# Two down products ahead of the first pieces, the inverse assembly at the head of iteration 0, and key products first in iteration 13

## The reference

```
x = x + attn(xn) + moe(xn)                   # xn = layernorm(x)
attn: q,k,v = split(silu(causal_conv1d(xn @ w_qkv)))   # 16 key heads, 32 value heads, 128 wide
      q,k = l2norm(q), l2norm(k);  beta = sigmoid(xn @ w_b)
      g = -exp(A_log) * softplus(xn @ w_a + dt_bias)
      per token: St = St*exp(g); St += k (v - k St) beta; o = q St
      o = o * rsqrt(mean(o^2)) * norm_weight * silu(xn @ w_z);  attn = o @ w_out
moe:  top 2 of 8 experts by xn @ router_w, each silu(g)*u @ w2, plus a shared expert of width 1024
```

## Time and profile before

| | us |
|---|---|
| median of 3 runs | 1095.32 (1089.68 to 1099.28) |
| profiled execution, whole | 1106.24 |
| its span | 1104.3 |
| TensorE busy | 1030.0 (93%) |
| VectorE busy | 800.5 (72%) |
| ScalarE busy | 633.9 (57%) |
| GpSimd busy | 519.3 (47%) |

### The profile page before, as it was taken

How to read it: one execution, slowest core, us unless ns; L and a number is a source line. 1 busy time by engine, 2 the same in 40 slices (tenths; PEclk the granted TensorE clock), 3 DMA queues, 4 the chain that set the end, 5 groups by cost and what they waited for, 6 DMA issues and landing times.

```text
span 1104.3 us, 22254 instructions
## 1 busy us (share of the span) xinstructions
PE 1030.0 (93%) x8190; PEld 789.7 (72%) x8190; DVE 800.5 (72%) x1469; ACT 633.9 (57%) x1176; POOL 519.3 (47%) x1140
## 2 busy tenths in 40 slices
PE   4889999999789999999999999999999999996897
PEld 4665666578476877777777778777777778783776
DVE  4552332275769898989889898989888988897444
ACT  4341222234557777666767576777767676774453
POOL 4500000266455557383847465564738374735610
PEclk9989999999879999999999999999999999998999
DMA  9933111151132333415152334233241514332121
GB/s 325 398 114 111 48 34 59 54 160 26 44 120 37 125 50 113 97 65 123 46 116 68 96 74 125 44 119 67 96 104 58 123 57 105 75 97 42 24 47 48
DMA packets 183513, 103.16 MB, mean 93 GB/s; under 512 B 155632, under 2 KB 169584, under 8 KB 180080
## 3 DMA queue, kind: packets, MB, share of 16 engines
q1 hardware_dynamic: 181872, 97.55, 32.1%
q0 software_dynamic: 1536, 4.20, 1.1%
HBM read 79.77 MB, written 21.95 MB: 92 GB/s over the span
## 4 chain that ended last, share of the span: by engine, by line
PE 57%; DVE 8%; ACT 7%; issue 4%; POOL 3%; DMA 1%; SPq 0%; ACTq 0%; DVEq 0%
PE rg L1585 9%; PE pj L1416 6%; PE pj L1418 5%; PE pj L1417 5%; PE rg L1568 5%; PE rg L1552 5%; PE rg L1486 4%; DVE nm L1294 3%; PE rg L1560 3%; PE rg L1569 2%; DVE shared_down_or_conv L1257 2%; ACT vn L1229 2%; ACT sqk L1183 2%; PE rg L1488 2%; PE rg L1531 2%
## 5 line engine op out<-in xcount | busy, mean ns | idle before, releaser
L1085 POOL TENSOR_TENSOR rows<-rows,shared_down_or_conv 128x126 f32<-128x126 f32 (+22 forms) x496 | 187.7, 378 | 239.1 <-DMA shared_down_or_conv<-n_scratch 201.5
L1257 DVE SCALAR_TENSOR_TENSOR shared_down_or_conv<-pj,taps,shared_down_or_conv 128x510 f32<-128x510 f32 x372 | 275.5, 744 | 27.5 <-ACT shared_down_or_conv L1135 18.8
L1088 POOL TENSOR_TENSOR rows<-rows 128x126 f32<-128x126 f32 (+22 forms) x496 | 194.8, 393 | 38.9
L1416 PE MATMUL pj<-xhi,whi 128*128 128x512 f32 x376 | 164.1, 437 | 2.4 <-POOL wlo L1065 1.4
L1294 DVE SCALAR_TENSOR_TENSOR nm<-rg,wneg,hidden_or_decays 128x512 f32<-128x512 f32 (+1 forms) x256 | 139.5, 609 | 15.9 <-PE rg L1488 14.1
L1418 PE MATMUL pj<-xhi,wlo 128*128 128x512 f32 x376 | 149.9, 399 | 0.0
L1417 PE MATMUL pj<-xlo,whi 128*128 128x512 f32 x376 | 149.8, 398 | 0.0
L1135 ACT ACTIVATE shared_down_or_conv<-pj,taps 128x512 f32<-128x512 f32 x124 | 85.0, 686 | 108.0 <-PE pj L1418 106.4
L1585 PE MATMUL rg<-wo,gated 128*128 128x256 f32 x512 | 130.6, 391 | 0.1
L1585 PEld LDWEIGHTS rg<-wo,gated 128*128 128x128 f32 x512 | 95.0, 192 | 15.1 <-issue 1.3
L1416 PEld LDWEIGHTS pj<-xhi,whi 128*128 128x128 f32 x376 | 71.5, 190 | 42.7 <-issue 24.4
(11 more groups left out here) (238 smaller groups left out, 1991.3 us busy)
## 6 DMA issues: line engine op xcount, KB each, us to landing
hidden_or_decays<-eg_scratch SPq DMA_DIRECT2D x16, 1536.0 KB, 8.0
wraw<-w_heads SPq DMA_DIRECT2D x16, 776.0 KB, 4.5
w1a<-w_up SPq DMA_DIRECT2D x9, 1024.0 KB, 7.7
shared_down_or_conv<-n_scratch SPq DMA_DIRECT2D x32, 256.0 KB, 4.0
w2a<-w_down SPq DMA_DIRECT2D x8, 512.0 KB
wo<-w_out SPq DMA_DIRECT2D x16, 256.0 KB
n_scratch<-nm SPq DMA_DIRECT2D x64, 64.0 KB
rt_scratch<-shared_down_or_conv SPq DMA_DIRECT2D x32, 128.0 KB, 2.3
```

What stands on the lines that cost most here:

```text
L1085: gp.tensor_tensor(tmp, rb[:, 0:r, t:t + 1].to_broadcast([P, r, w]), nb[:, t:t + 1, t + 1:].to_broadcast([P, r, w]), ALU.mult).then_inc(el ...
L1088: gp.tensor_tensor(rb[:, 0:r, t + 1:], rb[:, 0:r, t + 1:], tmp, ALU.add).then_inc(elim, 1)
L1257: v.scalar_tensor_tensor(out=y, in0=it.pbank[item][:, :, 0:S - s], scalar=taps[par][:, piece(j)[0], KS - 1 - s:KS - s], in1=y, op0=ALU.mul ...
L1416: te.matmul(bank, whi[par][w], xhi[:, k, cols], start=(k == 0), stop=False)
```

## The change

Three parts, each a reordering; no product is added or left out.

1. First block: `down(0)` and `down(1)` stand ahead of the four pieces on TensorE, `down(2)` behind them. On VectorE the softplus parts 1 to 3 leave the loop over products and stand behind it, with `add(0)` and `add(1)` between them, all ahead of the four convolutions.
2. Iteration -1: K comes earlier in TensorE's list; the scans and ScalarE's part of the decays of head 1 (D, E) come here from iteration 0. GpSimd gathers seven sets behind its weight split instead of three. Iteration 0: LA1 is first, the other assembly steps follow closely, the key products come behind them, MIX is VectorE's first item, and GpSimd gathers the last four sets ahead of its weight split.
3. Iteration 13: K0 to K3 stand ahead of LA1, and the output products come later. Iteration 14: SQ is TensorE's first item; Z2, OUT0 and Z3 come ahead of LA1; P4 and P5 stand behind K3 on VectorE.

```diff
--- before.py
+++ after.py
@@ -538,8 +538,8 @@
                         if n == 0:
                             locate()
                             assert count[0] == ROUTED, count
-                        elif n in (2, 5, 6, 7):
-                            softplus((2, 5, 6, 7).index(n))
+                        elif n == 2:
+                            softplus(0)
 
                     def turned_rows(j):
                         v.wait_ge(xt_full, j + 1)
@@ -584,11 +584,13 @@
                                                scalar=-1.0, in1=rk2[:].unsqueeze(2).to_broadcast([P, NT, REP]),
                                                op0=ALU.mult, op1=ALU.mult).then_inc(small, 1)
 
+                    softplus(1)
+                    add(0)
+                    softplus(2)
+                    add(1)
+                    softplus(3)
                     for q in range(4):
                         first_conv(q)
-                        if q == 1:
-                            add(0)
-                    add(1)
                     add(2)
                     turned_rows(0)
                     turned_rows(1)
@@ -739,10 +741,11 @@
                     te.matmul(pR[:, NT * E:2 * NT * E], every[:], either[:], start=True, stop=True).then_inc(counted, 1)
                     for n in range(1, NS):
                         up(n)
+                    for n in range(2):
+                        down(n)
                     for q in range(4):
                         first_project(q)
-                    for n in range(3):
-                        down(n)
+                    down(2)
                     turn_rows(0)
                     turn_rows(1)
                     down(3)
@@ -848,32 +851,33 @@
             LATER = {"G", "H", "DN"}
             OWN = {
                 -1: (
-                    ("K0 G0 K1 H0 G1 K2 H1 K3 P4 G2 H2 P5 G3 H3 P6 DN0 P7 DN1 G4 H4 P0 VT0 VT1 G5 H5 P1 VT2 VT3 G6 H6 P2 "
-                     "G7 H7 P3 DN2 DN3").split(),
-                    ("G0 W G1 P4 G2 P5 S4 G3 P6 S5 SK P7 S6 G4 S7 P0 VT0 VT1 G5 P1 S0 VT2 VT3 G6 P2 S1 G7 P3 S2 S3").split(),
-                    ("K0 K1 H0 K2 H1 K3 P4 H2 P5 H3 P6 DN0 P7 DN1 H4 P0 H5 P1 H6 P2 H7 P3 DN2 DN3").split(),
+                    ("K0 K1 G0 K2 H0 K3 G1 H1 P4 G2 H2 P5 G3 H3 P6 DN0 P7 DN1 G4 H4 P0 VT0 VT1 G5 H5 P1 VT2 VT3 G6 H6 P2 P3 "
+                     "G7 H7 DN2 DN3").split(),
+                    ("G0 W G1 P4 G2 P5 S4 G3 P6 S5 SK P7 S6 G4 S7 P0 VT0 VT1 G5 E0 P1 S0 E1 VT2 VT3 G6 E2 P2 S1 E3 P3 S2 G7 "
+                     "S3").split(),
+                    ("K0 K1 K2 H0 K3 H1 P4 H2 P5 H3 P6 DN0 P7 DN1 H4 D0 P0 D1 H5 D2 P1 D3 H6 P2 P3 H7 DN2 DN3").split(),
                 ),
                 0: (
-                    ("Z0 Z1 P4 P5 SQ Z2 K0 P6 Z3 K1 K2 P7 P0 LA1 K3 LA2 LB1 P1 LB2 U1_0 U1_1 N21_0 N21_1 P2 U2_0 U2_1 "
-                     "VT0 P3 O0 VT1 O1 VT2 O2 O3 VT3").split(),
-                    ("E0 Z0 P4 SQ Z1 S4 P5 S5 E1 P6 E2 W Z2 E3 SK S6 Z3 P7 LA1 LA2 S7 LB1 LB2 U1_0 U1_1 P0 P1 S0 U2_0 P2 "
-                     "U2_1 VT0 S1 O0 P3 O1 VT1 O2 S2 O3 VT2 S3 VT3").split(),
-                    ("D0 P4 D1 D2 P5 SQ D3 K0 P6 K1 K2 P7 K3 MIX N21_0 N21_1 P0 P1 P2 O0 P3 O1 O2 O3").split(),
+                    ("LA1 Z0 Z1 LA2 Z2 P4 LB1 SQ Z3 LB2 K0 P5 U1_0 U1_1 K1 N21_0 N21_1 P6 U2_0 K2 U2_1 K3 P7 O0 P0 O1 P1 "
+                     "VT0 O2 VT1 P2 O3 VT2 P3 VT3").split(),
+                    ("LA1 SQ Z0 Z1 LA2 Z2 P4 LB1 Z3 LB2 S4 W P5 U1_0 U1_1 SK S5 P6 U2_0 U2_1 S6 P7 S7 O0 P0 VT0 S0 O1 P1 "
+                     "VT1 O2 S1 P2 O3 VT2 S2 P3 VT3 S3").split(),
+                    ("MIX P4 SQ K0 P5 K1 N21_0 N21_1 P6 K2 K3 P7 P0 O0 P1 O1 O2 P2 O3 P3").split(),
                 ),
                 NG - 3: (
-                    ("SO Z0 P4 Z1 SQ Z2 K0 OUT0 K1 OUT1 Z3 OUT2 P5 P6 P7 LA1 K2 OUT3 LA2 K3 LB1 OUT4 OUT5 LB2 P0 OUT6 "
-                     "U1_0 U1_1 N21_0 P1 N21_1 U2_0 P2 U2_1 P3 VT0 OUT7 VT1 O0 O1 O2 O3 VT2 VT3").split(),
-                    ("SQ Z0 E0 Z1 P4 Z2 E1 SO Z3 P5 W E2 LA1 S4 E3 LA2 P6 LB1 S5 LB2 P7 S6 U1_0 P0 U1_1 SK S7 P1 U2_0 S0 "
-                     "P2 S1 U2_1 P3 VT0 VT1 S2 O0 O1 O2 O3 VT2 S3 VT3").split(),
-                    ("D0 SO D1 SQ P4 K0 OUT0 OUT1 D2 K1 D3 OUT2 P5 K2 OUT3 K3 P6 OUT4 OUT5 P7 OUT6 N21_0 P0 N21_1 P1 P2 "
-                     "OUT7 P3 O0 O1 O2 O3").split(),
+                    ("SO Z0 Z1 SQ Z2 K0 Z3 K1 P4 K2 P5 OUT0 K3 P6 LA1 OUT1 LA2 P7 LB1 P0 OUT2 LB2 OUT3 U1_0 U1_1 P1 N21_0 "
+                     "N21_1 OUT4 P2 U2_0 U2_1 OUT5 P3 OUT6 VT0 OUT7 VT1 O0 O1 O2 O3 VT2 VT3").split(),
+                    ("SQ E0 Z0 Z1 E1 Z2 E2 SO Z3 E3 P4 W LA1 P5 S4 LA2 P6 LB1 S5 LB2 P7 S6 U1_0 P0 U1_1 SK S7 P1 S0 U2_0 "
+                     "P2 U2_1 S1 P3 S2 VT0 S3 VT1 O0 O1 O2 O3 VT2 VT3").split(),
+                    ("D0 SO D1 D2 SQ K0 D3 K1 K2 K3 P4 P5 OUT0 P6 OUT1 P7 OUT2 OUT3 P0 N21_0 N21_1 P1 OUT4 P2 OUT5 P3 OUT6 "
+                     "OUT7 O0 O1 O2 O3").split(),
                 ),
                 NG - 2: (
-                    ("P4 Z0 SO SQ Z1 P5 K0 K1 K2 K3 LA1 Z2 OUT0 P6 OUT1 OUT2 Z3 OUT3 OUT4 LA2 P7 LB1 OUT5 OUT6 LB2 U1_0 "
+                    ("SQ Z0 SO Z1 P4 K0 P5 K1 Z2 K2 OUT0 K3 Z3 LA1 OUT1 OUT2 LA2 P6 OUT3 LB1 OUT4 OUT5 LB2 P7 OUT6 U1_0 "
                      "U1_1 N21_0 N21_1 OUT7 U2_0 U2_1 VT0 VT1 O0 O1 O2 VT2 VT3 O3").split(),
-                    ("P4 SQ SO E0 Z0 E1 S4 Z1 P5 E2 E3 LA1 S5 P6 Z2 Z3 LA2 SK LB1 LB2 U1_0 U1_1 U2_0 P7 S6 U2_1 S7 VT0 "
-                     "O0 O1 VT1 O2 VT2 VT3 O3").split(),
-                    ("D0 D1 SO P4 SQ D2 D3 K0 K1 K2 K3 P5 OUT0 P6 OUT1 OUT2 OUT3 OUT4 OUT5 OUT6 N21_0 N21_1 P7 OUT7 O0 "
+                    ("SQ SO E0 Z0 E1 Z1 E2 P4 E3 P5 Z2 S4 Z3 LA1 S5 LA2 P6 LB1 SK LB2 P7 S6 U1_0 U1_1 S7 U2_0 U2_1 VT0 "
+                     "VT1 O0 O1 O2 VT2 VT3 O3").split(),
+                    ("D0 SQ SO D1 K0 D2 K1 D3 K2 K3 P4 P5 OUT0 OUT1 OUT2 P6 OUT3 OUT4 OUT5 P7 OUT6 N21_0 N21_1 OUT7 O0 "
                      "O1 O2 O3").split(),
                 ),
                 NG - 1: (
@@ -894,7 +898,7 @@
 
                 def __init__(self, b, behind):
                     def present(order):
-                        return [i for i in order if kind(i) in LATER or not (b == -2 or b == -1 and (kind(i) in ("D", "E") or i == "SQ")) and (b <= NG - 3 and (b > -2 or i != "W") if i in EARLY else
+                        return [i for i in order if kind(i) in LATER or not (b == -2 or b == -1 and i == "SQ") and (b <= NG - 3 and (b > -2 or i != "W") if i in EARLY else
                                                      -1 <= b <= NG - 2 if kind(i) in FRONT else
                                                      b >= 1 if kind(i) in TAIL else 0 <= b <= NG - 1)]
 
@@ -1105,13 +1109,13 @@
                 def run(it):
                     if it.b == -1:
                         gather(range(0, 5))
+                    elif it.b == 0:
+                        gather(range(12, 2 * NT))
+                        gp.wait_ge(gathered, 2 * NT * 16)
                     if "W" in it.items_a:
                         split_lo(it.b + 2, it.odd, it)
                     if it.b == -1:
-                        gather(range(5, 8))
-                    elif it.b == 0:
-                        gather(range(8, 2 * NT))
-                        gp.wait_ge(gathered, 2 * NT * 16)
+                        gather(range(5, 12))
                     if "K3" in it.items_v:
                         eliminate(it.b + 1, it)
 
@@ -1184,7 +1188,7 @@
                                          ACT.Square).then_inc(sq_made, 1)
                         elif k == "E":
                             i = number(item)
-                            a.wait_ge(decay_made, 2 * B * n + 2 * i + 2)
+                            a.wait_ge(decay_made, 2 * B * max(n, 1) + 2 * i + 2)
                             for r in range(REP):
                                 a.activation(eg[:, r, i, S:EC], eg[:, r, i, S:EC], ACT.Copy,
                                              scale=eg[:, r, i, S - 1:S]).then_inc(cross_made, 1)
@@ -1340,7 +1344,7 @@
                         elif item == "SQ":
                             key_scales(n, it, par)
                         elif k == "D":
-                            decays(n, number(item))
+                            decays(max(n, 1), number(item))
                         elif k == "K":
                             decayed(n, par, number(item), it)
                         elif k == "N21":
```

## The result

The changed kernel takes 1118.64 us (median of 4 runs, 1112.66 to 1119.76), the kernel before beside it 1095.4: ratio 1.0193, 95% interval 1.0133 to 1.0253, 21 us slower by the ratio, 23 by the medians. Forecast was 1096.2, within 1086 to 1108. The profiled execution of the change is one of these 4 (1118.29, span 1116.3), while that of before stood 10.9 us above its others; the spans differ by 12.0 only. TensorE's clock was 0.974 of full in the mean, against 0.980.

The account below looks back on a forecast made before the run. TensorE was taken to bound nearly everything, with a second loop through K3 and the elimination nearly as long. First block +3.9, iterations -1 and 0 0, iterations 13 and 14 -3: +0.9 on 1095.3 gives 1096.2 us, range 1086 to 1108.

Parts of the forecast that it names:

- First block, forecast +3.9: First block: a later `turned_rows(0)` on VectorE and half clock on TensorE together cost 3.9 us, bounds +2.0 to +5.
- The two terms: First block: +2.0 us for VectorE's queue, `turned_rows(0)` at 78.0 instead of 76.03, and +1.9 for half clock behind TensorE's idling.
- Iterations -1 and 0, forecast 0: The stall goes from iteration 0 to LA1 of iteration 1; together -0.7 to +1.1 us, taken as 0.
- the -2.6 of its sum: LA1 of iteration 1 can't start before 351.1, against 353.7 in the old kernel: 2.6 us earlier.
- K3 hardly moves: Iteration 0: TensorE finishes some 11 us earlier, but K3 ends at 306 against 307.1.
- The rival's +7.4: Late K3 in iteration 0: without hold-ups the new list loses 5.4 us and 2 of clock; total 1104, chance 0.29.
- forecast 1.8 us longer: Elimination 0 on GpSimd, now beside decay scans: 62 operations at some 29 ns more each, +1.8 us.
- the forecast took 6.5 from the earlier trace: From an elimination's end to LA1: 6.5 us, the least between the two, read at head 14.
- Iterations 13 and 14, forecast -3: LA1 of iteration 15 comes 5.3 us earlier; 1.0 given back for LA2, 1.3 for half clock; bounds -5.3 and +1.
- The waits forecast at SQ and Z3: Iteration 14: TensorE idles 4 us at SQ for ScalarE's squares and 5 us at Z3 for P4's bank.
- K3 of iteration 13 ends about 8 us earlier: Iteration 13: early keys end elimination 14 at 1003 instead of 1011.3, removing the 8.37 us wait ahead of LA1.
- The carrying over: The profiled run is 10.9 us above the others' median; the same +0.9 us on 1095.3 gives 1096.2.

Follow-up runs that it names:

- the second profile of before: The kernel before, unchanged, profiled once more on the chip of the part runs; median 1096.4 us, span 1094.5, without the waits of its first profile.
- The mended kernel: Iterations -1 and 0 reordered anew against the kernel before: scans back in iteration 0, SQ and early keys ahead of LA1; 1100.4 us against 1107.6, ratio 0.9935.
- 13 alone: Only iteration 13 has the change's lists, all else as in the kernel before; 1099.3 us against 1095.3, ratio 1.0063.
- the first try at mending iteration 0: Change's iterations -1 and 0 only, with SQ and K0 to K3 early in iteration 0; 1098.6 us against 1095.3 before, ratio 1.0029.
- the first block alone: Only the first block is changed, all iterations have the lists of the kernel before; 1100.5 us against 1096.4, ratio 1.0040.

## Why the prediction was wrong

It failed in two steps, worth 8 and 10 us, and held in the first block.

**First block, forecast +3.9: right.** The part alone cost +4.1; against the second profile of before, `block_up` comes at 75.16 instead of 71.44, +3.7. VectorE's queue was the bound. The two terms came out otherwise than in the sum: without the hold-up VectorE is 8.5 us earlier than forecast (69.55 instead of 78.0), and TensorE idles 3.5 us instead of 10, against 1.0 before; that is +2.5 where the sum has +2.0. `down(3)` at a lower clock cost 1.1 of the 1.9. On the chip with the hold-up, where the forecast's premise holds, TensorE idled 7.0 us, `down(3)` took 5.9 us, and iteration -1 started 4.0 us later: the total held there too.

**Iterations -1 and 0, forecast 0: wrong, +8.0.** Counted from the start of iteration -1, the forecast has LA1 of iteration 1 at 133.3 us (351.1 - 217.8) against 135.95, the -2.6 of its sum. Measured are 139.35 against 131.05, +8.3. The step that failed is "K3 hardly moves", with the stall merely changing its place, and it failed on both sides.

The old list's side is 4.9 of the 10.9 us between forecast and measurement. I took K3's 307.1 and LA1's 353.7 of the earlier trace rows as what the old list gives; but K3 had waited in a hold-up that three of five chips don't have, and without it ends 83.5 instead of 89.3 us behind the start. I had this reading among the rivals, and the 10.9 us by which the profiled run stood above the others was the evidence for it. The rival's +7.4 for this part is near the 8.0, in part by luck: its K3 was right (301.3), but it had LA1 at 345.7, which is 127.9 us behind the start and not 131.0, and nothing for the new list's own lateness.

The new list's side is the other 6: LA1 of iteration 0 came 62.4 us after the start instead of 59.2, and K3 32.1 after LA1 instead of 29. Behind the wait of 4.24 us at LA1 of iteration 0 the clock was 0.50 up to 280 us: LA1 took 1.9 instead of 1.2 us and Z0 2.9 instead of 1.5, some 2 of the 3 us. The terms of the 62.4:
- Elimination 0 itself: forecast 1.8 us longer; its 31 pairs take 24.7 instead of 22.5 us, +2.2. The mended kernel, with the scans back in iteration 0, is at 22.5 again, so they are the cause. Here are GpSimd's groups, the change's first:
```profile
L1092 POOL TENSOR_TENSOR rows<-rows 128x126 f32<-128x126 f32 (+22 forms) x31 | 12.6, 405 | 2.4
L1089 POOL TENSOR_TENSOR rows<-rows,shared_down_or_conv 128x126 f32<-128x126 f32 (+22 forms) x31 | 12.1, 389 | 2.5 <-POOL rows L1082 0.2
```
```profile
L1088 POOL TENSOR_TENSOR rows<-rows 128x126 f32<-128x126 f32 (+22 forms) x31 | 11.5, 369 | 2.4
L1085 POOL TENSOR_TENSOR rows<-rows,shared_down_or_conv 128x126 f32<-128x126 f32 (+22 forms) x31 | 11.0, 355 | 8.3 <-DMA shared_down_or_conv<-n_scratch 6.0
```
 The Trainium skill, page SBUF — State Buffer, section Who interferes with whom, says that only the port pair which VectorE and GpSimd share causes contention, and that it is an exclusive lock. By that, an estimate: the four pairs of scans, 1.2 us each, would cost about 5. The rows show 2.2.
- From its end to LA1: 9.3 us, where the forecast took 6.5 from the earlier trace rows. Four gathers now go out right behind it, beside the loads that LA1 waits for. Loads of the inverse, issue to landing, from 262 to 278 us and then the same loads from 342 to 353 us, with no gathers beside them:
```profile
p<-rt_scratch SPq DMA_DIRECT2D x1, 64.0 KB, 4.8
```
```profile
p<-rt_scratch SPq DMA_DIRECT2D x1, 64.0 KB, 3.1
```
 That these gathers cause it was not tried by itself.

The idle time at LA1 of iteration 1 was forecast at 8 us and was 8.4. The clock behind it was forecast at 1.9 to 3.7 us; to LA1 of iteration 2 the change takes 53.5 and 54.9 us, where before, with no idle time there, takes 50.4 and 50.8, so 3 to 4. But it was no extra cost against the old kernel without hold-ups: that one waits 3.16 us at the same place and then takes 54.0.

**Iterations 13 and 14, forecast -3: wrong, +7.3 (10.1 by ratio).** The waits forecast at SQ and Z3 came in place and size (3.8 and 5.7 us). Even the gain forecast for iteration 14 came: from its start to LA1 of iteration 15 the change takes 68.5 us (1010.0 to 1078.57), the kernel before 73.5 (993.6 to 1067.09), -5.0 where the forecast had -5.3. The failed step is the one before it: "K3 of iteration 13 ends about 8 us earlier, ... and the 8.37 us are gone", with nothing counted for what moving K0 to K3 ahead pushes back. Iteration 13 is 12.1 us longer (62.6 instead of 50.5), and this term was missing from the sum. I followed K3's loop and never ScalarE's list of 13, where the taps of P5, P6 and P7 each stand behind a copy of LA1, LA2 or LB2, nor the result banks held by the OUT additions behind them. The wait of 8.9 us does go (13 alone: LA1 of iteration 14 waits 0.2 us), but it is paid for in iteration 13; and 14's list takes the same wait away once more.

**The carrying over.** A sum made on the profiled run and moved by its distance to the median holds only if that distance is spread evenly. Here it lay in two of the places that the change touches: 8.9 us at the start of iteration -1 and 4.9 more at LA1 of iteration 1, of which 3.6 came back as clock by LA1 of iteration 2.

## What to carry to other kernels

If the profiled run stands apart from the timed ones, profile the old kernel again before any stall in it is counted as a gain: a wait that other executions don't have is no room. When items are moved ahead in one engine's list, follow each other engine's list at that place for a short operation that has come to stand behind a long wait. Here it was taps behind copies in iteration 13, and copies behind S4 in the first try at mending iteration 0. With two loops of nearly equal length, a stall taken from one comes back as a wait for the other, and even a short wait of TensorE can cost more behind it, by the clock, than it lasts. Two edits that remove the same wait don't add up.

## What the runs showed of the hardware

- On two of the five chips used, beside DMAs that GpSimd issues, ScalarE's silu waited 8.6 to 10.1 us instead of 2.2, for a product that is long done by TensorE's rows; and TensorE's 64 small products of LA1 took 5.7 to 6.0 us instead of 1.2, with gaps of 0.3 to 1.2 us between them, and K3 waited 5.8 to 6.0 us on VectorE. The other three ran the same program without it, some 12 us (1.1%) faster.
- Beside four gathers, issued 1.0 us each, a 64 KB load landed after 4.8 instead of 3.1 us.
- TensorE ran at 1.2 instead of 2.4 GHz behind idle times of 8.4, 4.2 and even 2.65 us (10 us at a clock of 0.50, +3.4 us to the end). It isn't the same each time: at LA1 of iteration 1 the second profile of before idled 3.16 us and then took 54.0 us to the next LA1, the first block alone idled 3.08 and took 50.6 at full clock.
- Four pairs of VectorE's scans beside GpSimd's 62 operations of an elimination made these 2.2 us longer in all (24.7 instead of 22.5).
